# An attention loop on three engines: when the query shift is issued, how far the ring of maxima leads, in which order its row pairs come, and whether the last unit's sums are split

## The reference

```python
q = apply_rope(q); k = apply_rope(k); q = q * (1.0 / jnp.sqrt(jnp.float32(hd)))
scores = jnp.einsum('bhqd,bhkd->bhqk', q, k)
attn = jax.nn.softmax(scores, axis=-1)
out = jnp.einsum('bhqk,bhkd->bhqd', attn, v)
x = x + out @ Wo + bo            # then layer norm, feed-forward, residual
```

## Time and profile before

| | us |
|---|---|
| runs shown (3) | median 950.79, from 949.54 to 954.23 |
| profiled execution, its own time | 951.02 |
| its span, first to last instruction | 948.9 |
| attention loop, first reduction to the end of the last exponentials | 338.2 to 674.9 |
| busy over the span | PE 829.0 (87%), DVE 661.9 (70%), ACT 554.9 (58%) |

### The profile page before, as it was taken

The page is one execution under the profiler, slowest core; times in us unless marked ns, Lnnn a source line. Parts: engine busy times, 40 slices in busy tenths (PEclk is TensorE's granted clock), DMA queues, the critical chain, the costliest instruction groups (busy, mean ns, idle before and its releaser), DMA issues.

```text
span 948.9 us, 17393 instructions
## 1 busy us (share of the span) xinstructions
PE 829.0 (87%) x6621; PEld 530.8 (56%) x6621; DVE 661.9 (70%) x1288; ACT 554.9 (58%) x1205; POOL 197.5 (21%) x177
## 2 busy tenths in 40 slices
PE   5889937799999889999999999999995899895894
PEld 3579734599856543333332333333575598594694
DVE  5945883266477999999999999992427364566362
ACT  3442532255525856999999988899634254413252
POOL 0100037355500050000000000000112454204385
PEclk9999958899999999999999999999996799995898
DMA  4650001311130000000000000000230312000444
GB/s 122 192 151 1 2 14 53 114 57 35 38 88 1 1 1 1 2 1 2 1 2 2 1 2 1 1 2 1 93 87 15 94 37 73 1 1 31 125 38 69
DMA packets 54643, 36.86 MB, mean 39 GB/s; under 512 B 9138, under 2 KB 50162, under 8 KB 54546
## 3 DMA queue, kind: packets, MB, share of 16 engines
q1 hardware_dynamic: 47218, 25.98, 9.8%
q0 software_dynamic: 7344, 9.77, 4.4%
HBM read 22.31 MB, written 14.48 MB: 39 GB/s over the span
## 4 chain that ended last, share of the span: by engine, by line
PE 33%; DVE 32%; POOL 14%; issue 10%; ACT 4%; DMA 4%; SPq 1%; POOLq 0%; DVEq 0%; ACTq 0%
DVE arena L1635 22%; POOL slots L1148 7%; POOL results L1159 5%; PE psum L1719 4%; POOL results L1170 3%; PE psum L1688 2%; PE psum L1252 2%; ACT arena L1899 2%; PE psum L287 2%; PE psum L280 2%; PE psum L402 2%; PE psum L380 2%; PE psum L1782 2%; PE psum L1770 1%; PE psum L1617 1%
## 5 line engine op out<-in xcount | busy, mean ns | idle before, releaser
L1635 DVE TENSOR_REDUCE arena<-psum 128x2 f32<-128x1024 f32 x256 | 294.1, 1218 | 8.6 <-PE psum L1617 8.6
L1899 ACT ACTIVATE arena<-psum 128x512 f32<-128x512 f32 x512 | 266.7, 607 | 19.0 <-PE psum L1688 16.8
L1295 ACT ACTIVATE arena<-psum,arena 128x128 f32<-128x128 f32 x340 | 96.9, 368 | 122.4 <-PE psum L1262 65.6
L1719 PE MATMUL psum<-arena 128*32 128x256 f32 (+1 forms) x1920 | 159.6, 405 | 0.2 <-ACT expert_w L1880 0.2
L287 PE MATMUL psum<-la_wqkv,ident 128*128 128x384 f32 x342 | 127.3, 524 | 12.7 <-DMA la_bo<-in_L_attn_a_bo_dram 10.2
L1688 PE MATMUL psum<-arena 32*128 32x512 f16 x512 | 127.1, 385 | 1.8 <-ACT arena L1899 0.4
L1617 PE MATMUL psum<-arena 32*128 32x512 f16 x512 | 100.7, 385 | 17.2 <-DVE arena L1635 15.2
L287 PEld LDWEIGHTS psum<-la_wqkv,ident 128*128 128x128 f32 x342 | 66.7, 203 | 63.2 <-issue 15.8
L1148 POOL DMA_INDIRECT slots<-xn,arena x64 | 66.6, 1041 | 167.3 <-DVE arena L1372 148.7
L1252 PE MATMUL psum<-arena 128*128 128x128 f32 x680 | 96.8, 288 | 0.4 <-DVE arena L1453 0.3
L1262 PE MATMUL psum<-arena 128*128 128x128 f32 x680 | 90.2, 276 | 1.0 <-ACT arena L1295 1.0
(11 more groups left out here) (279 smaller groups left out, 1066.5 us busy)
## 6 DMA issues: line engine op xcount, KB each, us to landing
arena<-slots SPq DMA_DIRECT2D x19, 256.0 KB, 3.1
arena<-results SPq DMA_DIRECT2D x12, 256.0 KB, 4.2
slots<-blank SPq DMA_DIRECT2D x1, 2560.0 KB, 11.8
expert_w<-in_L_attn_b_w_dram SPq DMA_DIRECT2D x1, 2048.0 KB, 8.5
expert_w<-in_L_attn_b_w_dram SPq DMA_DIRECT2D x8, 256.0 KB, 4.8
expert_w<-in_L_ffn_W_dram SPq DMA_DIRECT2D x1, 2048.0 KB, 8.5
expert_w<-in_L_ffn_W_dram SPq DMA_DIRECT2D x8, 256.0 KB, 4.5
results<-arena POOLq DMA_INDIRECT x85, 2.3
```

Of the source, the lines that this page charges most:

```text
L1295: last = nc.scalar.activation(self.hT[:, p, c, :], ps[:, 2 + p, c * P:(c + 1) * P], self.func, bias=own[:, FF + c:FF + c + 1])
L1635: v.tensor_reduce(self.mx[:, h % 2, keys, qt, 2 * pair:2 * pair + 2], core.psum[:, 2 * slot:2 * slot + 2, :], AX.X, ALU.max).then_inc(self ...
L1719: last = nc.tensor.matmul(core.psum[32 * j:32 * j + 32, 7, cols], self.vs[:, b * TB + kt, HG * g + j, :], self.prob[:, k % self.PROBS, j, ...
L1899: nc.scalar.activation(self.prob[:, k % self.PROBS, j, :], core.psum[:, 4 + tile % self.SCORE_BANKS, :], ACT.Exp).then_inc(self.prob_in, 1)
```

## The change

It moves the first half of the shift from after wave 3 to after wave 4, lowers the ring's lead from 6 maxima to 5, gives pair 0 before pair 1 in the list of items, and makes the sums of the last unit whole (one part of 512 queries, where part 0 stood) instead of two parts.

```diff
-    AHEAD = 6
-    SHIFT_AT = (3, 6)
+    AHEAD = 5
+    SHIFT_AT = (4, 6)
...
-        parts = [(qt, pair, keys) for qt in range(4) for keys in range(2) for pair in (1, 0)]
+        parts = [(qt, pair, keys) for qt in range(4) for keys in range(2) for pair in (0, 1)]
...
+        at_once = kt == 0 or h == self.HALVES - 1
         if part == 0:
             pe.wait_ge(self.prob_in, self.tile_of["score", k, HG - 1] + 1)
             if kt == 0 and h:
                 pe.wait_ge(self.sum_out, h)
-        if kt == 0 and part == 1:
+        if at_once and part == 1:
             return
-        cols = slice(256 * part, 256 * part + 256) if kt else slice(0, 512)
+        cols = slice(0, 512) if at_once else slice(256 * part, 256 * part + 256)
         for j in range(HG):
             last = nc.tensor.matmul(core.psum[32 * j:32 * j + 32, 7, cols], self.vs[:, b * TB + kt, HG * g + j, :],
-                                    self.prob[:, k % self.PROBS, j, cols], start=(kt == 0), stop=(kt == TB - 1 and part == 1))
-        if part == 1 or kt == 0:
+                                    self.prob[:, k % self.PROBS, j, cols], start=(kt == 0), stop=(kt == TB - 1 and (part == 1 or at_once)))
+        if part == 1 or at_once:
             last.then_inc(self.wave_in, 1)
```

## The result

The changed kernel takes 947.28 us (median of 16 runs, 945.5 to 950.8), the kernel before 950.98 us (16 runs, 948.79 to 954.23). The ratio is 0.9963 (95% interval 0.9953 to 0.9974), that is 3.7 us less, and at 0.4% inside the half per cent that was called the same. Forecast were 946.5 and a range of 942.7 to 950.3, with the chance of "the same" put highest. The profiled execution took 947.07 us, its span is 945.2.

What follows compares the result with a forecast made beforehand. The prediction took a circle of waits through PE, ACT and DVE, 18.74 us a plain unit, as the bound. Its terms, -1.2 - 0.8 - 0.7 - 1.7 = -4.4 us, gave a median of about 946.5, range 942.7 to 950.3.

Steps and rivals of the forecast that it cites:

- Part 1: First shift moved after wave 4: one gap of 0.39 us becomes two adding to about 0.4, 0 in a plain unit.
- Part 2: Ring lead of 5 instead of 6: three effects, -1.2, -0.8 and -0.7 us.
- (a): Start of the loop: the first wave needs 21 maxima instead of 22, -1.2 us.
- (b): Units without output turns: the circle of waits loses a join, 0.09 us in each of nine periods, -0.8 us.
- (c): Four output-turn units: wave 2's order becomes 9, o, 10; five periods take 100.3 us instead of 101.0, -0.7.
- Part 3: Order of pairs: the swap keeps a wave's first fill on other array rows than its scores, 0 us.
- Part 4: Last unit: whole sums take 0.99 us instead of 1.14 and score 3 goes beside score 2, -1.7 us.
- the rest of the kernel only moves: Everything behind the loop keeps its durations, with 1 us allowed either way for its low-clock stretches.
- A: Plain units: DVE's gap of 0.39 us really closes in nine periods, giving 943.9 us; chance 0.18.
- B: Last unit: ACT waits at score 2 for all PE saves, only 0.2 us of the tail left, 948.1; chance 0.10.
- C: Wave 4 of turn units: turn, fill, score 2 and shift queue on PE, +4.8 us, slower at 952.1; chance 0.08.
- D: Circle unchanged, the moved shift merely swaps gaps, only start and last unit count: 948.1 us; chance 0.12.

Runs made afterwards that it cites:

- half_max: Changed kernel with every reduction over only the first 256 of 512 keys: plain unit 18.29 us, ratio to the kernel before 0.9818.
- sum_after_3: Changed kernel with the whole sum of wave 0 behind score 3 instead of ahead of it: plain unit 18.63 us, ratio to the kernel before 0.9971.
- fill_late: Changed kernel with wave 2's second ring fill behind scores 2 and 3, ahead of the sum: plain unit 18.64 us, ratio to the kernel before 0.9969.
- shift_back: Changed kernel with the first shift after wave 3 again: plain unit 18.66 us, turn unit 20.45, ratio to the kernel before 0.9969.
- only_shift: Kernel before with only the first shift moved after wave 4: plain unit 18.72 us, turn unit 20.04, ratio to the kernel before 0.9979.
- lead4: Changed kernel with a lead of 4 and pairs in the old order: plain unit 18.65 us, turn unit 21.03, ratio to the kernel before 0.9991.
- only_whole: Kernel before with only the last unit's sums made whole: last interval between copies 17.26 us for 19.05, ratio to the kernel before 0.9973.
- turns_first: Changed kernel with output turns one item earlier, ahead of maxima 9 and 13: turn unit 20.04 us, ratio to the kernel before 0.9927.
- pairs_back: Changed kernel with the pairs in the old order (1, 0): plain unit 19.40 us, ratio to the kernel before 1.0085.

## Why the prediction was right, point by point

**The bound.** Right: the circle of waits, read from the trace before, gave 11.28 to the second shift's fill and five pitches back, and both were found again. half_max shows that the circle goes through DVE. What I had not seen is how few ways lead out of it: sum_after_3 and fill_late each took out a link and found one of ACT's in its place.

**Part 1, the moved shift, 0 in plain units.** Right: two gaps of 0.2 for one of 0.39, and shift_back and only_shift give 0.01 and 0.02 a unit. Not seen in this term: with the old lead the move is worth 0.52 in each turn unit (only_shift). The prediction put the turn units under the lead, as one net number; it is two of opposite sign.

**Part 2.** (a) -1.2 forecast, -1.15 measured. (b) 0.09 a unit forecast, 0.09 measured. The join of eight items stands one item behind them in DVE's list, so a fill that waits for the ninth item goes ahead of it: the fill at 499.28 follows the reduction that ends at 499.23, not the next one, which stands behind the join. Nine periods were forecast as -0.8, and what the loop's 4.30 leaves after the other terms (1.15, 0.54, 1.78) is 0.83. So small a term could be luck in one kernel. It is not: lead4 and shift_back, which have no join in the circle either, have 18.65 and 18.66, and only_shift and only_whole, which have it, 18.72 and 18.73. (c) -0.7 forecast over five periods, measured -0.5 (100.97 to 100.43). ACT waits 0.85 and 0.68 around wave 2, where it had waited 0.17 and 0.68, and 0.59 at wave 4: these are the +0.65 at that point and the 0.56 of the forecast. turns_first shows what the order 9, o, 10 costs: 0.38 in each such unit.

**Part 3, the order.** Right: nothing as it stands, and 0.75 a unit if left out.

**Part 4, the last unit.** -1.7 forecast for the last copy, -1.79 measured (only_whole); a wave period of 2.7 forecast, 2.72 measured; a whole sum with 0.99 (663.41 to 664.41 is 1.00) and not 1.14. The exponentials ended 1.25 earlier within the unit, for 1.3 forecast. The formula that the prediction took from the Trainium skill (TensorE: Matmul & The Clock Gate, Back-to-back issue gap) is the one for a matmul by itself, and by it cost goes nearly with columns alone. It does not describe these sums: two parts of 256 columns took longer than one of 512. The Trainium skill's page TensorEngine Tiling (Array Packing), section Key Properties, says that a change of tiling mode drains the engine, and a split sum makes more such changes in a wave; the 0.15 by which two parts exceed a whole sum would agree with that, but no run here separates the drain from the rest. Wrong was one clause: that what follows is one chain on PE. The transposes behind the copy wait for DVE twice, 0.21 at their first weight load (675.10) and 0.25 further on (676.88). DVE's scaling and last divisions hang on ACT's square root, and that came only 3.92 earlier (672.33 for 676.25). The next stage on PE starts 3.96 earlier (677.34 for 681.30) and not 4.45.

**Sum.** -4.4 forecast; -4.3 in the loop, -3.7 in the span and in the medians. The step that was mis-sized is the last one, "the rest of the kernel only moves": 0.5 is the two waits just named, and a further 0.2 to 0.3 is lost in stages behind, where the traces of one and the same code differ by more than that.

**Rivals.** A falls: periods at 18.65, not 18.35. B falls: 1.79, not 0.2. C falls: its waits are there, 0.85 and 0.59, but ACT's waits of 0.44 and 0.51 of before are gone, so waves 4 and 5 hold 0.59 of idle time and not more than 1.10, and turn units became shorter. D falls as to the circle: 0.09 is the size of a rounding in one unit, but each of the eight plain periods is 0.08 to 0.10 shorter.

What stays open: how the rest of the kernel comes to vary by 6 us between executions, and why the turns cost more in lead4. A version with score 2, sum, second fill and then score 3 in wave 2, which might open the circle without a link of ACT's, was not tried.

## What to carry to other kernels

When three engines are each about 95% busy or more in a steady loop, read the period from a repeated instruction and follow one full circle of waits through all of them: the period is the circle's length, an edit that doesn't shorten it only moves a gap, and one small instruction taken out of it is worth its full length each time around. When a lead or an offset between two instruction streams changes, look at everything that was placed by position in either: here it was the order of pairs (0.75 us a unit if forgotten) and the output turns (0.38 us a turn unit, which the change left out). The same merging of two instructions can pay where its engine is the bound and cost where a neighbour is: whole sums gave 1.8 us in one unit and would have cost 1.8 in each of the others.

## What the runs showed of the hardware

Matmuls on different 32-row groups started within 0.01 us of each other (changed kernel, 510.56 and 510.57), and on the same rows 0.23 us apart (pairs_back). Two fills and two scores beside each other took TensorE 0.33 us until the sum started, the same four on shared rows 0.56. I had expected 0.2 more, and it was 0.23. Reducing half the elements took VectorE from 1217 to 690 ns, 57% and not half. If the time is a fixed part and one in proportion to the elements, the fixed part is about 0.16 us, an estimate from these two. Most of it overlaps the next reduction: one follows another every 1.131 us, and the half ones every 0.60 (two took 1.29 in half_max), by which about 0.07 is fixed.
